# A chunk's root on GpSimd and the place of the add to X on VectorE, in a state-space stage

## What is computed

```python
proj = hidden_states @ in_proj_w.T
gate, xBC, dt = jnp.split(proj, [INTER, INTER + CONV_DIM], axis=-1)
# causal convolution with 4 taps over xBC, then silu
y = _ssd(x, Bm, Cm, D, dt, dt_bias)      # selective scan in chunks of 128 tokens
yg = y * jax.nn.silu(gate)
yg_g = yg.reshape(Bsz, S, NG, GROUP)     # 8 groups of 1024 channels
rstd = jax.lax.rsqrt(jnp.mean(jnp.square(yg_g), axis=-1, keepdims=True) + EPS)
out = (yg_g * rstd).reshape(Bsz, S, INTER) * norm_w
return out @ out_proj_w.T
```

## Time and profile before

| | before |
|---|---|
| median of 3 runs | 3577.77 us (3572.93 to 3585.99) |
| the profiled execution, its own time | 3579.42 us |
| its span | 3577.5 us |
| busy: PE, DVE, ACT, POOL | 89%, 59%, 53%, 35% |
| mean granted clock of TensorE | 0.91 |

### The profile page before, as it was taken

The page is one execution under the profiler, slowest core; times in us unless marked ns, Lnnn a source line. Parts: engine busy times, 40 slices in busy tenths (PEclk is TensorE's granted clock), DMA queues, the critical chain, the costliest instruction groups (busy, mean ns, idle before and its releaser), DMA issues. The chain is left out here.

```text
span 3577.5 us, 49371 instructions
## 1 busy us (share of the span) xinstructions
PE 3166.5 (89%) x16025; PEld 1891.4 (53%) x16025; DVE 2114.4 (59%) x4295; ACT 1880.4 (53%) x4012; POOL 1267.0 (35%) x3220
## 2 busy tenths in 40 slices
PE   7999999999999999999999897658888788888779
PEld 4455455454454554544544544336666666666654
DVE  5356375385374562753853734767777777777640
ACT  2354363452542633534525422588888888888721
POOL 1033052050240330510502410176666666666400
PEclk9999999999999999999999998767777877777889
DMA  2222132131221231321311201000000000000010
GB/s 85 59 80 94 48 97 89 49 111 65 68 92 59 89 100 36 102 81 53 113 59 51 77 9 43 1 1 1 1 1 1 1 1 1 1 1 1 1 46 24
DMA packets 65795, 169.55 MB, mean 47 GB/s; under 512 B 11777, under 2 KB 19329, under 8 KB 64513
## 3 DMA queue, kind: packets, MB, share of 16 engines
q1 hardware_dynamic: 54448, 115.17, 10.1%
q10 hardware_dynamic: 11088, 51.19, 4.2%
HBM read 161.08 MB, written 5.24 MB: 46 GB/s over the span
## 5 line engine op out<-in xcount | busy, mean ns | idle before, releaser
L1702 ACT ACTIVATE X<-ah_z,ah_trial 128x256 bf16<-128x256 f32 (+6 forms) x896 | 732.3, 823 | 25.1 <-POOL ah_trial L1805 14.0
L735 PE MATMUL m_ps_y<-hT,m_w_proj 128*128 128x512 f32 x1152 | 508.0, 594 | 8.4 <-DVE m_xbc L1027 8.4
L735 PE MATMUL m_ps_x<-hT,m_w_proj 128*128 128x512 f32 x1152 | 506.1, 592 | 0.0
L879 POOL TENSOR_TENSOR m_xdec<-m_xdt,m_decay_out 128x512 f32<-128x512 f32 x112 | 129.2, 1154 | 1041.1 <-DVE m_xdt L1044 1029.3
L954 ACT ACTIVATE m_mix<-m_mix,m_cs 128x128 f32<-128x128 f32 x1024 | 312.9, 388 | 267.7 <-DMA m_mix<-cs_rows 267.7
L1657 PE MATMUL ah_ps_o<-a_v,X 128*128 128x17 f32 x2304 | 354.1, 282 | 44.6 <-DVE hT L1902 44.6
L735 PEld LDWEIGHTS m_ps_y<-hT,m_w_proj 128*128 128x128 f32 x1152 | 218.7, 191 | 280.6 <-issue 271.4
L1657 PEld LDWEIGHTS ah_ps_o<-a_v,X 128*128 128x128 f32 x2304 | 338.9, 220 | 51.9 <-ACT X L1713 49.8
L735 PEld LDWEIGHTS m_ps_x<-hT,m_w_proj 128*128 128x128 f32 x1152 | 218.2, 190 | 271.2 <-issue 271.2
L1044 DVE TENSOR_TENSOR m_xdt<-m_ps_y,m_dt 128x512 f32<-128x512 f32 x128 | 87.1, 681 | 408.0 <-PE m_ps_y L768 408.0
L1713 ACT ACTIVATE X<-ah_ps_e 128x512 f32<-128x512 f32 (+3 forms) x384 | 185.8, 485 | 194.0 <-PE ah_ps_e L1644 130.7
(11 more groups left out here) (245 smaller groups left out, 6039.2 us busy)
## 6 DMA issues: line engine op xcount, KB each, us to landing
m_mix<-cs_rows SPq DMA_DIRECT2D x128, 512.0 KB, 4.4
m_w_proj<-in_w_proj ACTq DMA_DIRECT2D x69, 512.0 KB, 3.2
m_fade<-fade_rows SPq DMA_DIRECT2D x224, 128.0 KB, 2.9
m_w_out<-in_w_out ACTq DMA_DIRECT2D x7, 2048.0 KB, 7.8
X<-in_x SPq DMA_DIRECT2D x8, 256.0 KB, 6.2
m_w_out<-in_w_out SPq DMA_DIRECT2D x1, 2048.0 KB, 10.5
x_away<-X SPq DMA_DIRECT2D x1, 2048.0 KB, 10.7
X<-x_away SPq DMA_DIRECT2D x8, 256.0 KB, 5.6
```

The source lines that it names most:

```text
L735: last = pe.matmul(pair[i % 2][:, half], w_proj[:, n % RING, k, (i % 2) * P:(i % 2 + 1) * P], hT[:, k, half * BANK:(half + 1) * BANK], sta ...
L1702: act.activation(sign[:, at % 2, 0:(t + 1) * P], z[:, h % RING, cols(t)], ACT.Sign, bias=trial[:, h % RING, 0, t - 1:t], scale=-1.0, accum ...
```

## The change

Two edits in `mamba`. On GpSimd the root is a small function, `root_of(c)`, called at the head of an even unit from 4 on for the chunk two before, and twice behind the loop; the call at the end of the odd unit is gone. On VectorE `add_out` of an even unit stands behind `outputs` of that unit and no longer ahead of it.

```diff
                 decayed(0)
+                def root_of(c):
+                    pool.wait_ge(ms_done, g * NT + c + 1)
+                    pool.wait_ge(added, g * NT)
+                    pool.tensor_tensor(rstd[:, c:c + 1], ms[:, c:c + 1], env.minus_half[:, 0:1], ALU.pow).then_inc(rstd_done, 1)
+
                 for u in range(NU):
                     c, half = u // 2, u % 2
                     U = g * UG + u
+                    if u >= 4 and half == 0:
+                        root_of(c - 2)
                     if 0 < c < NT - 1:
                         pool.wait_ge(off_done, off_at(g, u))
                         pool.wait_ge(state_done, state_at(g, u - 2))
...
                         pool.tensor_tensor(square_all[:], square_sum[:, 0], square_sum[:, 1], ALU.add).then_inc(chunk_summed, 1)
-                    if u >= 3 and half:
-                        pool.wait_ge(ms_done, g * NT + c)
-                        pool.wait_ge(added, g * NT)
-                        pool.tensor_tensor(rstd[:, c - 1:c], ms[:, c - 1:c], env.minus_half[:, 0:1], ALU.pow).then_inc(rstd_done, 1)
-                pool.wait_ge(ms_done, g * NT + NT)
-                pool.tensor_tensor(rstd[:, NT - 1:NT], ms[:, NT - 1:NT], env.minus_half[:, 0:1], ALU.pow).then_inc(rstd_done, 1)
+                root_of(NT - 2)
+                root_of(NT - 1)
...
                 for u in range(NU):
                     if u + 1 < NU:
                         inputs(g, u + 1)
+                    outputs(g, u)
                     if u >= 4 and u % 2 == 0:
                         add_out(g, u // 2 - 2)
-                    outputs(g, u)
                     if u >= 3 and u % 2 == 1:
                         mean_square(g, u // 2 - 1)
```

## The result

| | before | after |
|---|---|---|
| median | 3578.8 us (6 runs, 3572.93 to 3585.99) | 3513.03 us (6 runs, 3509.64 to 3516.87) |
| ratio to before | | 0.9815 (95% interval 0.9802 to 0.9827) |
| the profiled execution, its own time | 3579.42 us | 3513.40 us |
| its span | 3577.5 us | 3511.6 us |
| mean granted clock of TensorE | 0.910 | 0.911 |

The change gives 65.8 us, 1.8%. The forecast was 3522 us, 56 us less than before, with a range down to 3514. The direction holds, and so does the cause that was named for the stalls; the gain is 10 us larger than the sum, as the sum had left a cost of the stalls out, and the time lies 1 us outside the range.

The account below looks back on a forecast made before the run. The prediction took TensorE to bound each group: 45.7 us of listed waits, 40 x 0.24 and 0.6 for unit 4 made 55.9 us, so 3579.4 became 3523.5, or 3522 us as the median. Range 3514 to 3546 us.

Parts of the forecast that it names:

- the sum: TensorE's stalls in the scans: 55.9 us to get back, taken from 3579.4 us; 3522 us as the median.
- What bounds: Each group is tied to TensorE; the change can win what TensorE waits in the scans.
- The price of a stall: TensorE's pairs of steps: 13.93 us without a stall, 15.13 in the pair shown; 55.9 us in all.
- 45.7 + 40 x 0.24: TensorE's 40 waits at L782: 45.7 us listed plus 0.24 each for covered transposes and slower restart, 55.3 us.
- GpSimd's part: The root's new place on GpSimd leaves the instruction order as it was; costs nothing and gives nothing.
- VectorE's margins: VectorE with `outputs` ahead of the add: everything over 1 us in hand, load 13.2 us against TensorE's 13.93 a pair.
- The first pass: Steps 8 and 9 reworked: PSUM reads end 1.87 us before TensorE wants them; 2.1 us in hand for the bank.
- Collisions with GpSimd: VectorE's L1074, L1077 and L1046 may lengthen beside GpSimd's work: up to 15.47 us a pair, 13.2 taken, costing nothing.
- The second rival: VectorE becomes the bound through collisions with GpSimd; 14.7 us a pair gives 3553 us; chance 0.12.
- The slower rival: ScalarE's square behind later decays and a `mix` load; 8 us later gives 3596, below 6.5 costs nothing; chance 0.04.
- The third rival: The wait for `rstd` only moves; with the root at t + 11, TensorE waits for mix: about 3578; chance 0.04.
- The range: 3514 to 3546 us: up to 8 us below for spread and clock, above the same and part of VectorE becoming bound.

Follow-up runs that it names:

- experiment 2: GpSimd's edit alone on the kernel before, VectorE's order as before: 3579.77 us, ratio 1.0002 to before.
- Experiment 6: Changed kernel with six waited-for copies of a PSUM bank on VectorE ahead of `outputs(14)`, once a group: 3545.75 us, ratio 0.9906 to before.
- experiment 4: Changed kernel with the add back ahead of `outputs` in units 4 to 12, behind it only in unit 14: 3550.54 us, ratio 0.9919 to before.
- experiments 7 and 8: Changed kernel with one or two more adds into a spare tensor per even unit from 4 on, on VectorE: 3518.8 us and 3547.66 us.
- Experiment 9: Changed kernel with GpSimd's root of chunk c-2 moved to the end of even unit 2c: 3607.23 us, ratio 1.0072 to before.

## Why the prediction was right or wrong

- **What bounds.** Right. The projections kept their time, and the scans lost what TensorE had waited. 102 of VectorE's 126.8 us of waiting went, and they were worth 66 us.
- **The price of a stall.** Right as far as it goes: 13.91 us a pair measured, 13.93 forecast. But the step "45.7 + 40 x 0.24", by which a stall costs its length and 0.24 us of restart and nothing else, is the one that failed. I took the clock of a whole scan, 1.00, for that of every stretch in it, and looked at group 1, which lost no clock. In 4 of 8 groups the 2 to 3 us stall of step 15 was followed by some us at the lower clock: 6.4 us that the sum had at nothing, and 9.7 us in 5 of 8 groups in the trace of experiment 2, with the old order on VectorE. With the 6.4 and the 0.8 of the odd steps the forecast of 3522 would have been 3515, inside the range; the last 2 us are within what the runs spread. Experiment 6 shows it by putting a stall back, experiment 4 by taking only this one away. The table of stretches would have shown it before: 0.99 in three of seven periods, and 237.3 us of matmuls for 235.7.
- **GpSimd's part.** Right: experiment 2 gives 1.0002.
- **VectorE's margins.** The first pass was right. For the steady pace the pair's load was 13.2 us in the forecast, and it is 13.23 in one pair (491.79 to 505.02 for the start of `inputs`) and 14.04 in the next, about TensorE's pace. In the units 4 to 12 of group 1 the add ends at 8.3 to 9.2 us after the step's start, not 7.4, so 1.2 to 2.1 us were in hand, not 3. This term of mine was too good, with no effect on the sum; by experiments 7 and 8 the edge lies between one and two more adds of 0.67 us.
- **Collisions with GpSimd.** The median of L1077 (L1074 in the earlier trace rows) went from 693 to 1227 ns, and GpSimd's `xdec` and fade from 1154 and 1056 to 1306 and 1234 ns in the mean. In the pair shown after the change L1077 starts at 508.66, under GpSimd's fade (508.31 to 509.37), and ends 0.55 us behind it; L1080 starts at 509.95, under `xdec` (509.33 to 510.84), and ends 0.54 us behind that. On VectorE instructions with one input in SBUF kept their time (L1047, L1067 and L1087, 0.68 us). On GpSimd the later sums of squares got longer as well (887 to 975 and 454 to 578 ns), while the first got shorter (920 to 784). The rule of the Trainium skill (SBUF — State Buffer, Who interferes with whom), by which the later of two such instructions waits for the other's end, fits these times. The second rival did not come in, but it was nearer than its 0.12 says.
- **The slower rival.** Its mechanism exists, at the place named (the bank of `output(2c)`). Experiment 9 makes the root 6.9 us later in its step and gets 3607, and there the square does stand behind the decays and their `mix` load, as this rival says. From which lateness on it costs (6.5 us in the prediction) no run shows. The third rival had such a root, at t + 11, at 3578 with TensorE waiting for `mix`; at t + 11.2 it was 3607, with TensorE waiting for the bank.
- **The range.** It let the unknown clock cost only upwards. The lower end had 8 us for run-to-run spread and nothing for a saving that the stalls hid.

## What to carry to other kernels

A wait of one engine is worth what the bounding engine feels of it, plus what its idleness does to its clock: compare the busy time of like stretches before adding up stalls, since the same matmuls with more busy time tell of a lower clock. When an instruction that waits is moved behind others, ask whose buffer it frees: here the bank that the add clears became the next edge. An edit that only names another place in a program may leave the stream as it was; read the stream, not the diff.

## What the runs showed of the hardware

- The stalls of step 15, 1.8 to 3.0 us long, were sometimes followed by the lower of TensorE's two clock levels and sometimes not: in 4 of 8 groups of the kernel before, 5 of 8 in experiment 2 and 6 of 8 in experiment 6. There is no order by length: 1.92 and 2.01 us lost it, 2.27, 2.39 and 2.84 did not. The loss was 1.6 to 1.7 us of time in most cases and 3.3 in two (group 5 of experiment 2, group 4 of experiment 6).
- It isn't bound to the end of a scan. In experiment 9 it was lost in the middle of scans too, behind stalls of 1.58 to 2.50 us.
- Stalls of 0.5 to 1.5 us in the middle of a scan were not seen to lose it in the kernel before and in the experiments 2 and 4; neither was one of 2.00 us in experiment 4.
- What decides within the longer ones no run here settles.
